# Two key tiles at a time in the second attention layer of a two-layer transformer block

## The reference, cut to what matters

```python
x = x + _L1_xattn_ref(_layernorm(x), ctx_512, ...)

q_big = einsum('bshk,hkq->bshq', (hidden_q @ Wq.T).reshape(b, s, H, K), w_kc_q)
q_r   = einsum('bshq,hqr->bhsr', q_big, W_qr)
k_r   = einsum('bld,hdr->bhlr', kv_rope, W_kr)
attn  = softmax(einsum('bhsr,bhlr->bhsl', q_r, k_r), axis=-1)
ctx_c = einsum('bhsl,bld->bhsd', attn, kv_rope)
out   = einsum('bhsd,hkd->bshk', ctx_c, w_kc_kv).reshape(b, s, H * K) @ Wo.T
```

## Time and profile before

| | |
|---|---|
| runs of the kernel before | median 3187.75 us of 3 (3183.57 to 3194.1) |
| the profiled execution | 3174.48 us |
| its span, first to last instruction | 3172.7 us |
| PE busy, in the span | 2859.5 us (90%) |
| DVE, ACT, POOL busy | 1959.1, 1181.8, 1668.2 us |
| second layer's loop, the stretch that the change touches | about 1864 to 2826 us of the span |

### The profile page before, as it was taken

How to read it: one execution, slowest core, us unless ns; L and a number is a source line. 1 busy time by engine, 2 the same in 40 slices (tenths; PEclk the granted TensorE clock), 3 DMA queues, 4 the chain that set the end, 5 groups by cost and what they waited for, 6 DMA issues and landing times. The chain is left out here.

```text
span 3172.7 us, 42691 instructions
## 1 busy us (share of the span) xinstructions
PE 2859.5 (90%) x15992; PEld 1636.7 (52%) x15992; DVE 1959.1 (62%) x2330; ACT 1181.8 (37%) x1648; POOL 1668.2 (53%) x935
## 2 busy tenths in 40 slices
PE   7689999989999999996899979999999999986998
PEld 6544445444544454443788844444454454435665
DVE  3386667676766686754666466655655655636664
ACT  3124441445144423442333234444443443433331
POOL 0267766767667775772200047677676666741111
PEclk9689999999999999998999989999999999997999
DMA  8233331334123322322000043332223232300000
GB/s 288 86 92 80 80 103 34 80 80 105 45 66 83 94 67 55 80 52 88 1 1 1 21 90 79 72 73 68 69 70 72 66 74 64 83 29 25 6 6 12
DMA packets 98869, 209.17 MB, mean 66 GB/s; under 512 B 30306, under 2 KB 74322, under 8 KB 91116
## 3 DMA queue, kind: packets, MB, share of 16 engines
q1 hardware_dynamic: 98668, 206.44, 25.0%
HBM read 135.36 MB, written 46.00 MB: 57 GB/s over the span
## 5 line engine op out<-in xcount | busy, mean ns | idle before, releaser
L1129 POOL TENSOR_TENSOR sums<-sums,prob 125x896 f32<-125x896 f32 x556 | 1177.1, 2117 | 282.5 <-ACT prob L1069 239.5
L1216 DVE TENSOR_REDUCE maxpart<-pair 112x2 f32<-112x1000 f32 x744 | 889.5, 1196 | 449.5 <-PE pair L931 448.9
L1069 ACT ACTIVATE prob<-wide 125x896 f32<-125x896 f32 x768 | 704.4, 917 | 902.9 <-PE wide L957 898.9
L971 PE MATMUL single<-prob,kv 125*64 125x448 f32 x3072 | 753.6, 569 | 0.5
L952 PE MATMUL wide<-qhigh,kparts 64*125 64x448 f32 x3072 | 448.8, 369 | 1.5 <-DVE maxpart L1216 1.5
L931 PE MATMUL pair<-kparts,qhigh 64*112 64x500 f32 x1488 | 360.9, 481 | 86.1 <-DVE maxpart L1216 84.7
L931 PEld LDWEIGHTS pair<-kparts,qhigh 64*112 64x112 f32 x1488 | 130.2, 172 | 517.9 <-DVE maxpart L1216 438.6
L1129 POOL TENSOR_TENSOR sums<-prob 125x896 f32<-125x896 f32 x64 | 134.7, 2104 | 362.3 <-ACT prob L1069 362.3
L952 PEld LDWEIGHTS wide<-qhigh,kparts 64*125 64x125 f32 x3072 | 281.7, 184 | 79.7 <-issue 48.2
L957 PE MATMUL wide<-shift,ones_row 64*125 64x448 f32 x1536 | 284.8, 365 | 5.1 <-DMA shift<-maxrow 5.0
L952 PE MATMUL wide<-qlow,kparts 64*125 64x448 f32 x1536 | 283.3, 363 | 0.0
(11 more groups left out here) (329 smaller groups left out, 3919.9 us busy)
## 6 DMA issues: line engine op xcount, KB each, us to landing
kparts<-keys_merged SPq DMA_DIRECT2D x64, 750.0 KB, 8.9
kparts<-kparts SPq DMA_DIRECT2D x96, 250.0 KB, 3.1
keys_merged<-kparts SPq DMA_DIRECT2D x32, 750.0 KB, 7.3
recip<-zrec_merged SPq DMA_DIRECT2D x124, 112.0 KB, 2.8
w_low_values<-w_merged SPq DMA_DIRECT2D x64, 192.0 KB, 2.4
raw<-in_ctx SPq DMA_DIRECT2D x32, 375.0 KB
values_merged<-kv SPq DMA_DIRECT2D x32, 375.0 KB
kv<-values_merged SPq DMA_DIRECT2D x32, 375.0 KB
```

The costliest lines, as they stand in the source:

```text
L971: mm = pe.matmul(mix_acc[64 * half:64 * half + DC, 0:HQ], kv[:, b % 3, t, :], prob[:, (b * LT + t) % NPROB, half * HQ:(half + 1) * HQ], st ...
L1069: nc.scalar.activation(prob[:, n_ % NPROB, :].rearrange("p (a b) -> p a b", a=2), acc[0:LP, :, 0:HQ], ACT.Exp)\
L1129: nc.gpsimd.tensor_tensor(dst, first_in, prob[:, n_ % NPROB, :], ALU.add).then_inc(s["pool_sum"], 1)
L1216: V.tensor_reduce(maxpart[:, b % 2, t:NMAX:4, third], acc[0:TQ, :, 0:LB], AX.X, ALU.max).then_inc(*R.signal_drained(kind, *key))
```

## The change

In the second layer's loop the unit is now a pair of key tiles, p of 6, in place of one tile, t of 12. Before, a tile's steps were: score of t, mix of t-1, the maximum for four tiles ahead. Now a pair's steps are: a maximum, both scores, the second maximum, and then both mixes of the pair before. The other steps of a batch stand once a pair: `spread` and `share` at the end of the fifth and the sixth pair, `maxneg` and `maxT` in the fifth, ahead of `spread`; `norm` at the second; the two `square` steps together; `rstd` in the last two pairs with `xsplit` behind it; the `query` steps two a pair, one ahead of the mixes and one behind; `project` in three pairs. Nothing that is computed changes, and neither do the engines' codes for a step.

```diff
+    def ahead(b, t):
+        n = t + EARLY_MAX
+        due = (b + 1, n) if n < LT else (b + 2, n - LT)
+        if due[0] < NB:
+            maximum(*due)
+
     for b in range(NB):
         g, j = divmod(b, BG)
-        for t in range(LT):
-            ahead = (b + 1, t + EARLY_MAX) if t + EARLY_MAX < LT else (b + 2, t + EARLY_MAX - LT)
-            if t == 2 and b + 2 < NB:
+        for p in range(LT // 2):
+            t = 2 * p
+            if p == 1 and b + 2 < NB:
                 add("fetch", b + 2)
-            add("score", b, t, region=t % 2)
-            if b + 1 < NB and t == 8:
+            ahead(b, t)
+            add("score", b, t, region=0)
+            add("score", b, t + 1, region=1)
+            if b + 1 < NB and p == 4:
                 add("maxneg", b + 1)
-            if t or b:
-                old = (b, t - 1) if t else (b - 1, LT - 1)
-                add("mix", *old)
-                if not t:
+            ahead(b, t + 1)
+            queries = g + 1 < G and j == BG - 2 and p < NPAIR // 2
+            if queries:
+                add("query", g + 1, t, region=3)
+            if p or b:
+                old = (b, t - 2) if p else (b - 1, LT - 2)
+                add("mix", old[0], old[1])
+                add("mix", old[0], old[1] + 1)
+                if not p:
                     add("context", b - 1)
-            if t == 1 and b:
+            if p == 1 and b:
                 add("norm", b - 1, region=3)
-            if b + 1 < NB and t == 9:
+            if b + 1 < NB and p == 4:
                 add("maxT", b + 1, region=3)
...
+            if queries:
+                add("query", g + 1, t + 1, region=3)
+            if g and j == 1 and 1 <= p <= 3:
+                for m, half in (((0, 0),), ((0, 1),), ((1, 0), (1, 1)))[p - 1]:
+                    add("project", g - 1, m, half, region=None if half else 3)
             if g + 1 < G and j == BG - 3:
-                if t == 2:
+                if p == 1:
                     add("mean", g + 1, region=3)
-                if t in (3, 4):
-                    add("square", g + 1, t - 3)
-                if t == 5:
+                if p == 2:
+                    for k in range(KT):
+                        add("square", g + 1, k)
+                if p == 3:
                     add("var", g + 1, region=3)
-                if t in (7, 8):
-                    add("rstd", g + 1, t - 7)
-                if t == 10:
+                if p >= 4:
+                    add("rstd", g + 1, p - 4)
+                if p == 5:
                     add("xsplit", g + 1)
...
-            if ahead[0] < NB:
-                maximum(*ahead)
-            if t == 8 and b:
+            if p == 4 and b:
                 add("spread", b - 1)
-            if t == 10 and b:
+            if p == 5 and b:
                 add("share", b - 1, 2)
+    add("mix", NB - 1, LT - 2)
     add("mix", NB - 1, LT - 1)
```

More of the change, by code:

```diff
@@ L130, in rolling_schedule @@
                 add("maxT", b + 1, region=3)
-            if g and j == 1 and t in (2, 3, 5, 6):
-                m, half = divmod((2, 3, 5, 6).index(t), 2)
-                add("project", g - 1, m, half, region=None if half else 3)
+            if queries:
[3 more added lines that the diff above has]
+                    add("project", g - 1, m, half, region=None if half else 3)
@@ L143, in rolling_schedule @@
-                if t == 10:
+                if p >= 4:
+                    add("rstd", g + 1, p - 4)
+                if p == 5:
                     add("xsplit", g + 1)
-            if g + 1 < G and j == BG - 2 and t < NPAIR:
-                add("query", g + 1, t, region=3)
-            if ahead[0] < NB:
-                maximum(*ahead)
-            if t == 8 and b:
+            if p == 4 and b:
                 add("spread", b - 1)
-            if t == 10 and b:
+            if p == 5 and b:
```

## The result

The changed kernel takes 3246.8 us (median of 4 runs, 3236.63 to 3251.56), the kernel before on the same chip 3188.56 (4 runs, 3183.57 to 3194.1). The ratio is 1.0178, 95% interval 1.0148 to 1.0208: slower, by 47 to 66 us. The forecast was 3218 us in a range of 3150 to 3285.

A forecast was written before the change was run, and what follows sets the result against it. PE was taken as the bound, busy 934.9 of 962 us in the loop, plus its waits for the maximum. Terms -67 + 55 + 11 + 8 + 23 = +30 us on 3187.75 gave 3218 us, range 3150 to 3285.

The forecast's parts named there:

- Pairs: PE's loop: fewer passages between 64-row and all-row matmuls, a pair 3.89 us against 4.24, -67 us (-46 to -86).
- The passage from a maximum to a mix: PE, second maximum to mix in a pair: no row existed; bounded by 0.20 and 0.42 us, taken as 0.31.
- `maxT` ahead of `spread`: SP's order delays reads, `share` and later maxima: PE waits 2.5 us in 26 batches, net +55 us (+47 to +68).
- the margin of 0.35 us: Forecast gap between the end of `share` on DVE and POOL's first add of the next batch.
- a rival with 0.10: `share` lands behind POOL's add, PE waits 4.9 us in all 26 batches: +129 us, 3317 us; chance 0.10.
- the old wait of 0.42: PE's wait for the next maximum but one in the kernel before, put down to DVE waiting 0.76 us for reads.
- The norm's batches: DVE's norm steps in the fifth and sixth pairs of three batches make PE wait 8.5 us each: +11 us (0 to +18).
- The queries: A pair's second query right ahead of the next first maximum: 0.66 us, four times in three batches, +8 us (0 to +12).
- The clock: Half of 26 PE idles of 2.5 us followed by a fall to 0.50, 1.8 us each: +23 us (0 to 60).

The follow-up runs named there:

- e3: The kernel before, one tile at a time, with each mix two tiles behind its score instead of one, `context` and `norm` a tile later: 3186.89 us, ratio 1.0004.
- e4: The changed kernel, with POOL's first add of a batch waiting until the last `share` given to DVE is done: 3239.5 us, ratio 1.0147 to the kernel before.
- e2: The kernel before, in single tiles, with only SP's order changed, `spread` right behind `maxT`: 3270.47 us, ratio 1.025.
- e6: The changed kernel with `share` moved to POOL and SP's order left as changed: 3138.97 us, ratio 0.9859 to the kernel before.
- e1: The changed kernel with `spread` moved ahead of `maxT` in the fifth pair: 3179.1 us, ratio 0.997 to the kernel before.
- e5: e1 with `share` moved from DVE to POOL, into the next batch's first pair: 3131.98 us, ratio 0.9841 to the kernel before.

## Why the prediction was right, and which term was too small

**Pairs: -67 forecast, -61 measured.** A pair takes 3.92 to 3.95 us and not 3.89; the 61 is what the table leaves over, and the starts alone (two tiles 4.25 in most of the old loop, a pair 3.92) give 192 x 0.33 = 63. The passage from a maximum to a mix, for which no row existed, came out at the 0.31 chosen. e3 excludes slack as the source, and the `rest` column gives the same gain in four other kernels.

**`maxT` ahead of `spread`: +55 forecast, +74 measured.** This is the step that was mis-sized. Of the 26 ordinary batches 17 waited 2.25 to 2.50 us, 40.5 us together, as forecast. The other nine waited 4.75 each, 42.8 us, where the forecast put down 2.5. Together 83.2, less the old 9.4: 24 waits of 0.34 to 0.42, 21 of them behind a `share` and three in the queries' batches. The working had the margin of 0.35 us in it, and called the mechanism beyond it a rival with 0.10 that would take all batches or none. It took nine, as in these the reads came 1 to 1.9 us later than in the others. In e4, without the add on POOL, the same nine waits come to 33.4 us in place of 42.8: so of the 20 us that they lie above the forecast, about 9 are the add, and the rest the late reads alone, which no term priced. e2 and e6 show the term from two sides: SP's order alone, without pairs, costs 82 us in the loop, and with `share` off DVE some 2 us.

One reading of the working was wrong without harm. It put the old wait of 0.42 in the earlier trace rows down to the reads. But `share` takes 1.09 there in place of 0.61, and in 24 of the 26 ordinary batches of the kernel before it ran beside an add of POOL and ended 0.48 behind it. So in these the end of that add, and not the reads, set when the next maximum came free.

Why nine? The DMA traffic of the batch at 2112.13, from 2112 to 2117, and of the undisturbed one at 2143.23, from 2143.2 to 2147.5 (GB/s in 40 slices; kind of queue: packets, MB, share; then the issues with KB and median us to landing):

```profile
GB/s 0 0 0 0 0 0 0 0 0 0 0 86 129 172 143 172 158 186 201 246 143 115 115 43 0 0 0 14 14 0 14 14 0 0 0 0 0 0 0 0
...
q8 instruction: 1, 0.02, 1.3%
...
recip<-zrec_merged SPq DMA_DIRECT2D x2, 112.0 KB, 3.3
```

```profile
GB/s 0 0 0 0 0 0 0 0 0 0 0 0 100 167 167 134 133 150 233 167 233 167 150 150 133 33 17 0 0 0 0 0 0 0 0 0 0 0 0 0
...
recip<-zrec_merged SPq DMA_DIRECT2D x2, 112.0 KB, 2.8
```

In the first a packet of 16 KB of another queue, whose kind the profile calls "instruction", runs amid the 128 packets of the reads. In eight batches of the loop with a maximum behind `share` it is there; it started 2.05 to 2.8 us behind the issue and lasted 0.9 to 1.6 us. In these the second of the two reads lands in 3.8 to 4.4 us, in all others of them in 2.7 to 3.0 (the median of the two reads, 3.3 above, hides it: the first lands in 2.7 to 2.9 as always). The slices show how: the traffic stops, and the last four packets of the read, 1.8 KB or 14 GB/s in a slice, come 0.4 us later. In all eight the first of these four starts with the end of the 16 KB packet, to 0.02 us. These eight are eight of the nine waits of 4.75; in the ninth (issue at 2650.65) SP issued the reads 1.85 us later behind its store than otherwise. A packet of that queue began 1.14 us behind that store too, but in the kernel before one at 1.22 left a store alone (reads 1.37 behind it), so there the cause stays open.

The other traces agree. In the nine of this document, 31 batches each, such a packet began 1.8 to 2.8 us behind the issue 34 times, and the second read landed in 3.55 to 4.5 us every time. In 14 batches the packet began at most 0.8 us behind the issue or just ahead of it, and the landings are mixed, 2.7 to 3.7; in the other 231 the read landed in 2.65 to 3.2. In the kernel before, one such packet started 0.77 us behind the issue and cost nothing (2.75), and one at 0.40 (3.66) left PE's wait at 0.42. No run took the packet away, so its part is read from the times of the packets and not shown by experiment.

**The rule of the port.** The Trainium skill (SBUF — State Buffer, "Who interferes with whom") says that a DVE instruction with two inputs in SBUF contends with a GpSimd instruction that reads SBUF, and that the pair of ports which the two engines share is an exclusive lock that the one that issues first holds for the whole instruction. The traces agree in both orders: `share` 0.46 us ahead of the add took 0.63, and 0.65 us behind it 1.91, to 0.49 past the add's end; in e1 it took 2.08, to 0.48 past it. An add that started 0.33 us behind `share`, while that still ran, took 2.23 in place of 2.07.

**The norm's batches: +11 forecast, +3.8 measured** (19.3 us against 15.5). The forecast took DVE's operations there at the lengths of the kernel before, where POOL's adds ran beside some of them: the 1.56 of `x_n` in the earlier trace rows is a mean of 2.5 behind an add and 0.62 alone. In the new order `x_low` (1.09 in place of 2.25) and the second `x_n` run while POOL is idle, and the first `x_n`, at 2300.70, starts 0.1 us before an add ends and takes 0.62 too.

```profile
2305.78 0.62 DVE L1190 TENSOR_TENSOR x_n<-x_cen,x_std 128x448 f32<-128x448 f32 x1
...
2307.42 1.09 DVE L1195 TENSOR_TENSOR x_low<-x_n,x_high 128x896 fp32r<-128x896 f32 x1 [1.02 <-ACT x_high L1040]
```

**The queries: +8 forecast, +5.9 measured**, twelve waits of about 0.49. **Not priced:** `mean` (L890) and `project` (L1019) now follow `norm` in its region of PSUM and wait until ACT has read its total, three times 0.64 us each: 3.8 us. The start of the loop adds 1.3.

**The clock: +23 forecast, +29 measured.** 17 stretches at 0.50 against 3, each of 3.4 or 6.8 us. That the size is near is in part luck. The forecast let half of 26 waits of 2.5 us be followed by a fall. Of the 17 waits of 2.25 to 2.50 only three were; the other stretches start in or behind all nine waits of 4.75, the three of 3.5 in the norm's batches, and two of the three of 1.9 there. The nine alone account for 41 us at 0.50, 20 us of loss. In e2, on the other hand, 17 of 29 waits of 1.9 to 2.6 us were followed by a fall. So no share can be carried from one kernel to another, and why the two differ stays open. e5 and e6, without the waits of the ordinary batches, have 3 such stretches and 13.7 and 10.2 us at 0.50.

The terms in sum: -61 + 73.8 + 3.8 + 5.9 + 3.8 + 1.3 + 29 = +56.6, against 56.8 in the loop; with the 5 us outside it, the 62 between the profiled spans. The medians lie 58 apart. Of the 27 us that the forecast missed in the loop, 19 are the term of `maxT`, 6 each the pairs and the clock, 5 what was not priced, and -9 the norm's batches and the queries, which by luck made up for part of the rest. The range held, though the bounds of the terms, added up, give 3149 to 3300 and not the 3175 to 3280 that the prediction names.

## What to carry to other kernels

An edit in the order of one queue is priced by what stands behind its last consumer: here two DMAs let PE wait only because the maxima of later tiles are queued on DVE behind the one operation that reads them, and moving that operation later and to an engine with a gap took the loss in the ordinary batches away and left the gain. When a term rests on a margin (0.35 us between `share` and an add), compare the margin with the scatter of the same duration over all batches, and split the term by how many fall on either side, in place of one chance for all or none. Even that has a limit: in the kernel before, one batch in 29 had a late read (3.66 us), in the changed one eight of 29, since a change that moves a transfer also moves what it meets. And durations of an operation taken from a trace contain what ran beside it; if the change moves its neighbour away, they no longer hold.

## What the runs showed of the hardware

- Where a packet of 16 KB on a queue of kind "instruction", 0.9 to 1.6 us long, began 1.8 to 2.8 us behind the issue of two reads of 112 KB, the second read landed in 3.55 to 4.5 us in place of 2.65 to 3.2, in 34 cases of 34 over nine traces.
- An operation of DVE with two inputs that takes 0.62 to 0.63 us alone took 1.91 and 2.08 behind an add on POOL, and ended 0.49 and 0.48 us behind it. The same work on POOL took 1.13.
- Between matmuls of 64 rows and of all rows a passage cost about 0.16 us, an estimate: 61 us in the loop for two passages fewer in each of 192 pairs (61 / 384).
- The granted clock fell to 0.50 (1.2 GHz) for 3.4 or 6.8 us behind three of 17 waits of TensorE of 2.25 to 2.50 us in one kernel, and behind 17 of 29 of 1.9 to 2.6 us in another (e2).
